# A fused attention and expert layer: the weighted sum over expert products moves from ScalarE and GpSimd to VectorE

## The chip, the cores and the metric

The kernel runs on one core of a Trainium2 chip. The metric is the device time of one execution in microseconds (us). Before the change three runs took 1968.68, 1968.94 and 1974.44 us; the median is 1968.94 us.

## The reference

For each of 16 sequences of 512 tokens with 128 channels, in fp32, the layer takes a layer norm `xn` of `x` and returns `x + attn(xn) + ffn(xn)`. Both branches hold an attention with 16 heads of 8 channels over all 512 tokens; the one in the second branch turns q and k by their position ("rope" below, the other is "plain"). The second branch then norms its own residual stream to `x1` and sends that through a shared expert and a routed sum:

```
shared = swiglu(x1 @ W_shared_in) @ W_shared_out
p_expert = softmax over the 4 experts of the best group * that group's probability
w[token, e] = p_expert for the 2 best experts of the token, else 0       # 8 experts
h = swiglu(x1 @ W1_shared)
routed = sum over e of (h @ W2_experts[e]) * w[:, e]
out = rmsnorm(x1 + shared + routed)
```

The change touches the last sum, `routed`: all eight products are computed, scaled by the token's weight and added.

## The kernel before, in words

**Passes.** The program is unrolled. For each batch `b` it runs an even pass and an odd pass of 64 quarters each (a quarter is one head times one block of 128 tokens). In each quarter TensorE issues one score product (L550) and one "shift" product (L565: the scores again, with the row's maximum taken off) of another attention. Behind every fourth quarter it issues a value product (L585). VectorE takes the row maximum of each score product straight from PSUM (L857, `maximum`); ScalarE exponentiates each shift product (L693, `weigh`) into `weights`, which has room for 8 heads. The even pass of batch b scores its plain attention and weighs the rope attention of b-1; the odd pass scores the rope attention of b and weighs the plain attention of b. Scores go through three PSUM banks, so score t needs the maximum of t-3 done.

**Clips.** The plain weights are clipped. GpSimd clips 12 of the 16 heads (L1048, 128x2048 in one instruction); VectorE clips heads 3, 7, 11 and 15, each in two halves of 128x1024 (L865) behind the maxima of quarters 17 and 18, 33 and 34, 49 and 50 of the odd pass and of quarters 1 and 2 of the next even pass.

**Side jobs.** All other products share one PSUM bank, `side_ps`. The lists EVEN and ODD say behind which quarter TensorE issues which job; each job waits until the one before it has been read out of the bank. In the even pass these are mostly the up and down products of the experts' hidden layer; in the odd pass `exp0` to `exp7`, two for each block of 128 tokens, each holding 4 experts x 128 channels (L657). LAG says for which batch: the experts run two batches behind the scores, so 14 odd passes have both (batches 2 to 15), and the last two sets of experts run behind the scores' end.

**Experts before.** When `expN` is done, ScalarE scales its four 128x128 quarters by the gate column into `spread` (L727, `weight_experts`: two in one quarter, two in the next, and the last frees the bank). GpSimd adds them up in three instructions (L1110, L1113, L1115, `mix`) into `out_sb`.

**Order.** Each engine runs its own queue in the order in which the program was written. AT says in which quarter the small steps stand (`invert`: the softmax denominators, L873 and L875; `top`, `shares`: the router's steps on VectorE; `square_x1`, `square_out`: VectorE's row sums of squares, L884). GpSimd's order is written out in its functions `even` and `odd`. A GpSimd step that belongs to the experts' result is the router (L1073 to L1102), which gives `gate`; `root` (L1032, L1035) gives the inverse root mean square; `third` (L1147) is the last part of a split of q or k into bf16 parts; `place_v` (L1024) and `divide` (L1133) serve the attention.

Of the kernel before, what the change touches and what calls it, by code (L numbers as in the profile page):

```python
# [39 lines left out]
NT = S // 128  # L40
# [22 lines left out]
EVEN = [("v0", [1]), ("x1T", [3]), ("max_rope1", [5]), ("v1", [8]), ("gates", [11]), ("up0", [13]), ("down0", [18]),  # L63
        ("up1", [21]), ("down1", [26]), ("up2", [28]), ("down2", [33]), ("up3", [36]), ("down3", [41]),
        ("shared_out", [45]), ("max_plain0", [49]), ("y_plain", [53])]
ODD = [("xnT", [0]), ("q_plain", [4]), ("k_plain", [9]), ("max_plain1", [11]), ("exp0", [14]), ("exp1", [17]),
# [9 lines left out]
AT = {"merge": 40, "invert": 28, "hi0": 8, "hi1": 11, "mid0": 11, "mid1": 24, "copy1": 18, "copy0": 52, "z": 28,  # L76
      "shares": 36, "top": 27, "square_x1": 47, "scale_x1": 53, "square_out": 5, "scale_out": 16, "stats": 36,
      "moments": 49, "act_x1T": 0, "act_max_rope1": 0, "act_up": 0, "act_max_plain0": 1, "act_v": 1,
      "act_max_plain1": 0, "act_xnT": 1, "act_q_plain": 1, "act_q_plain_2": 3, "act_k_plain": 0,
      "act_k_plain_2": 2, "act_exp": 0, "act_max_rope0": 0, "dve_gates": 0, "dve_up": 2, "dve_down": 1,  # L80
      "dve_y_plain": 1, "dve_shared_out": 0, "dve_q_plain": 2, "dve_k_plain": 1, "dve_y_rope": 3, "dve_job": 1,
      "act_exp_gap": 1}
# [66 lines left out]
def layer_kernel(nc, x, wq, wkcT, wk, wvcT, wvp, wvr, wo, w_up, w_out, w2, w_gate, bias, norms, consts, out):  # L149
    ctx = ExitStack()  # L150
    with ctx:
        def sb(name, shape, dt=F32):
            return ctx.enter_context(nc.sbuf_tensor(name, shape, dt))

        def sem(name):
            return ctx.enter_context(nc.semaphore(name))
# [79 lines left out]
        spread = sb("spread", [128, 2, 4, 128])  # L236
        two = sb("two", [128, 2, 128])
        one = sb("one", [128, 128])
# [76 lines left out]
        mixed = sem("mixed")  # L315
        rms_used = [sem("rms_used_x1"), sem("rms_used_out")]
# [367 lines left out]
        def _(act):  # L684
# [33 lines left out]
            def weight_experts(b, n, half):  # L718

                if live(b, -2):  # L720
                    if half == 0:
                        full(act, b, f"exp{n}")
                        act.wait_ge(route, cnt(b, -2, ROUTE_A + ROUTE_B, ROUTE_A + ROUTE_B))
                        if n >= 2:
                            act.wait_ge(mixed, cnt(b, -2, 24, 3 * (n - 2) + 1))
# [70 lines left out]
            def odd(b):  # L796
                for t in range(UNIT):
# [11 lines left out]
                    for n in range(8):  # L809
                        for half in range(2):  # L810
                            if t == after("odd", f"exp{n}", AT["act_exp"]) + AT["act_exp_gap"] * half:
                                weight_experts(b, n, half)
# [23 lines left out]
        def _(dve):  # L836
# [103 lines left out]
            def odd(b):  # L940
                for t in range(UNIT):
# [34 lines left out]
        def _(pool):  # L976
# [128 lines left out]
            def mix(b, n):  # L1105

                if live(b, -2):
                    taken(pool, b, f"exp{n}")
                    taken(pool, b, "shared_out")
                    pool.tensor_tensor(two[:], spread[:, n % 2, 0:2, :], spread[:, n % 2, 2:4, :],  # L1110
                                       ALU.add).then_inc(mixed, 1)
                    pool.wait_ge(mixed, cnt(b, -2, 24, 3 * n + 1))
                    pool.tensor_tensor(one[:, :], two[:, 0, :], two[:, 1, :], ALU.add).then_inc(mixed, 1)  # L1113
                    pool.wait_ge(mixed, cnt(b, -2, 24, 3 * n + 2))
                    pool.tensor_tensor(out_sb[:, n // 2, :], out_sb[:, n // 2, :], one[:, :], ALU.add).then_inc(mixed, 1)  # L1115
                    pool.wait_ge(mixed, cnt(b, -2, 24, 3 * n + 3))
# [63 lines left out]
            def even(b):  # L1180
                split_max(b, "max_rope1")
                square_out(b)
                turn(b, 0)
                turn(b, 1)
                rope_less_first(b, 0, q_rest, q_parts)
                root(b, -3, 1)
                rope_less_first(b, 1, k_rest, k_parts)
# [3 lines left out]
                third(b, 0, ROPE, 1, k_rest, k_parts)  # L1191
                split_max(b, "max_plain0")
                router(b, False)
                place_v(b, PLAIN)
                divide(b, PLAIN)
                spread_of_x(b)

            def odd(b):
                clip(b, 0)
                split_max(b, "max_plain1")  # L1200
                clip(b, 1)
                clip(b, 2)
                mix(b, 0)
                third(b, 1, PLAIN, 0, q_rest, q_parts)
                third(b, 1, PLAIN, 1, k_rest, k_parts)
                mix(b, 1)
                clip(b, 4)
                mix(b, 2)
                clip(b, 5)
                mix(b, 3)  # L1210
                mix(b, 4)
                clip(b, 6)
                clip(b, 8)
                divide(b, ROPE)
# [69 lines left out]
```

## Time and profile before

| | |
|---|---|
| median of three runs | 1968.94 us |
| profiled execution | 1971.31 us, its span 1969.5 us |
| TensorE busy | 1798.6 us (91%) |
| VectorE busy | 1633.5 us (83%) |
| ScalarE busy | 1446.3 us (73%) |
| GpSimd busy | 1180.6 us (60%) |
| chain that ended last, by engine | PE 55%, DVE 27%, SP's queue 7% |
| mean granted TensorE clock | 0.979 |

In the profile PE is TensorE, PEld its weight loads, DVE VectorE, ACT ScalarE, POOL GpSimd, SP the queue that issues transfers; L857 is line 857 of the kernel before. A busy time is a union of the instructions' spans. Instructions of one engine may overlap: VectorE's maxima take 0.68 us each and start 0.60 us apart.

### The profile page before, as it was taken

To read this page: it belongs to the slowest core of one execution; us is meant where nothing else is said; L and a number is where in the kernel's file an instruction comes from. 1 tells how busy PE (TensorE), PEld (TensorE's weight loads), DVE (VectorE), ACT (ScalarE), POOL (GpSimd) and SP (SyncE) were. 2 spreads that over 40 slices of the span, in tenths; PEclk is the share of its full clock that TensorE was granted. 3 is DMA by queue.
4 is the path that set the end of the run, shared out by engine and by line. 5 is a ranking of instruction groups with operands and counts; after the bars stand their busy time and mean duration, and the time that the engine had idled before them with its cause. 6 is when DMAs were issued, how large, how long until landed. Compare 5 with 4: busy or idle time off the path is not lost.

```text
span 1969.5 us, 33956 instructions
## 1 busy us (share of the span) xinstructions
PE 1798.6 (91%) x10244; PEld 526.8 (27%) x10244; DVE 1633.5 (83%) x2741; ACT 1446.3 (73%) x3095; POOL 1180.6 (60%) x1759
## 2 busy tenths in 40 slices
PE   5888899999999999999999999999999999999964
PEld 1122222222222232222222232222222222222222
DVE  4999998979899898989889898989989898987110
ACT  1378777778787788788777788777778887877622
POOL 3344548466674847567584856657485666738244
PEclk9899999999999999999999999999999999999977
DMA  4122222212122221212222121212222121220100
GB/s 123 31 64 73 72 70 59 76 56 84 57 63 76 60 80 56 84 57 71 70 58 81 57 81 57 82 57 59 81 61 78 56 85 57 62 69 28 45 25 6
DMA packets 120255, 126.34 MB, mean 64 GB/s; under 512 B 35196, under 2 KB 86780, under 8 KB 119932
## 3 DMA queue, kind: packets, MB, share of 16 engines
q1 hardware_dynamic: 119112, 123.39, 21.0%
q8 instruction: 81, 1.33, 0.3%
q10 hardware_dynamic: 960, 0.79, 0.2%
q14 instruction: 102, 0.84, 0.1%
HBM read 29.11 MB, written 22.02 MB: 26 GB/s over the span
## 4 chain that ended last, share of the span: by engine, by line
PE 55%; DVE 27%; SPq 7%; issue 4%; DMA 3%; ACT 3%; POOL 1%; POOLq 0%; ACTq 0%; DVEq 0%
DVE negmax L857 18%; PE score_ps L550 15%; PE o_ps L585 13%; PE side_ps L657 13%; SPq L394 6%; PE side_ps L644 4%; DVE weights L865 2%; PE side_ps L626 2%; PE side_ps L630 2%; PE side_ps L614 1%; DMA res_old<-res_new 1%; PE shift_ps L565 1%; PE side_ps L649 1%; DVE hidden L902 1%; PE side_ps L600 1%
## 5 line engine op out<-in xcount | busy, mean ns | idle before, releaser
L857 DVE TENSOR_REDUCE negmax<-score_ps 128x1 f32<-128x512 f32 x2048 | 1293.5, 681 | 167.5 <-PE score_ps L550 160.2
L693 ACT ACTIVATE weights<-shift_ps 128x512 f32<-128x512 f32 x2048 | 1114.2, 604 | 273.6 <-PE shift_ps L565 249.6
L550 PE MATMUL score_ps<-kt,qt 48*128 48x512 bf16 x2048 | 670.0, 394 | 74.6 <-DVE negmax L857 55.7
L565 PE MATMUL shift_ps<-qt,kt 51*128 51x512 bf16 x2048 | 655.8, 387 | 8.5 <-DMA qt<-max_rows 5.3
L585 PE MATMUL o_ps<-weights,vt 128*32 128x512 f32 x4096 | 551.4, 611 | 0.4 <-POOL weights L1048 0.4
L1048 POOL TENSOR_SCALAR weights<-weights 128x2048 f32<-128x2048 f32 x192 | 366.0, 1906 | 207.6 <-ACT weights L693 189.6
L550 PEld LDWEIGHTS score_ps<-kt,qt 48*128 48x128 bf16 x2048 | 148.7, 94 | 850.0 <-DVE negmax L857 746.8
L657 PE MATMUL side_ps<-w_sb,hidden 128*128 128x512 f32 x512 | 255.7, 622 | 18.6 <-ACT spread L727 14.0
L727 ACT ACTIVATE spread<-side_ps,gate 128x128 f32<-128x128 f32 x512 | 159.5, 372 | 134.2 <-PE side_ps L657 132.4
L644 PE MATMUL side_ps<-x1T,w_up_sb 128*128 128x512 f32 x256 | 151.7, 676 | 16.0 <-DVE hidden L902 8.6
L565 PEld LDWEIGHTS shift_ps<-qt,kt 51*128 51x128 bf16 x2048 | 150.3, 94 | 43.3 <-ACT weights L693 30.8
L1110 POOL TENSOR_TENSOR two<-spread 128x256 f32<-128x256 f32 x128 | 97.1, 759 | 97.2 <-ACT spread L727 59.7
L865 DVE TENSOR_SCALAR weights<-weights 128x1024 f32<-128x1024 f32 x128 | 137.0, 1071 | 0.0
L585 PEld LDWEIGHTS o_ps<-weights,vt 128*32 128x32 f32 x4096 | 81.3, 108 | 171.5 <-issue 159.3
L657 PEld LDWEIGHTS side_ps<-w_sb,hidden 128*128 128x128 f32 x512 | 87.4, 190 | 137.7 <-issue 62.6
L1115 POOL TENSOR_TENSOR out_sb<-out_sb,one 128x128 f32<-128x128 f32 x128 | 62.9, 491 | 10.0
L778 ACT ACTIVATE tanh<-side_ps 128x512 f32<-128x512 f32 x64 | 38.7, 605 | 36.0 <-PE side_ps L644 36.0
L1113 POOL TENSOR_TENSOR one<-two 128x128 f32<-128x128 f32 x128 | 58.2, 455 | 10.0
L626 PE MATMUL side_ps<-xnT,wq_sb 128*128 128x512 f32 x96 | 57.8, 686 | 2.8 <-DVE q_rest L954 1.4
L902 DVE SCALAR_TENSOR_TENSOR hidden<-tanh,side_ps 128x512 f32<-128x512 f32 x64 | 43.4, 679 | 20.3 <-ACT tanh L778 20.3
L1041 POOL TENSOR_TENSOR out_sb<-out_sb,norm_sb 128x512 f32<-128x512 f32 x16 | 20.4, 1275 | 64.0 <-ACT out_sb L737 64.0
L644 PEld LDWEIGHTS side_ps<-x1T,w_up_sb 128*128 128x128 f32 x256 | 39.7, 196 | 69.5 <-DVE hidden L902 36.0
(108 smaller groups left out, 1407.5 us busy)
## 6 DMA issues: line engine op xcount, KB each, us to landing
qt<-q_parts SPq DMA_DIRECT2D x768, 32.0 KB
kt<-k_parts SPq DMA_DIRECT2D x744, 32.0 KB
o_rows<-o_sb SPq DMA_DIRECT2D x64, 256.0 KB, 2.0
swung<-turned SPq DMA_DIRECT2D x64, 128.0 KB, 2.4
heads_raw<-o_rows SPq DMA_DIRECT2D x64, 128.0 KB
inv_wide<-inv_rows SPq DMA_DIRECT2D x32, 256.0 KB, 3.3
x_in<-in_x_dram SPq DMA_DIRECT2D x16, 256.0 KB, 3.5
xn_mid<-xn_new SPq DMA_DIRECT2D x16, 256.0 KB, 3.4
```

The source lines that it names most:

```text
L394: eng.dma_start(to[a][row:row + 8, 4 * gh:4 * gh + 4, :], parts[a][c:128:4, part[t], :]).then_inc(qk_landed[a][gh], 16)
L550: pe.matmul(score_ps[:, score_bank(a, t), :], qt[a][row:row + HROWS, slot, 128 * tile:128 * tile + 128], kt[a][row:row + HROWS, slot, :], ...
L565: pe.matmul(shift_ps[:, shift_bank(a, t), :], kt[a][row:row + HROWS + MROWS, slot, 128 * tile:128 * tile + 128], qt[a][row:row + HROWS + M ...
L585: mm = pe.matmul(o_ps[32 * j:32 * j + 32, :], vt[a][:, tile, 4 * (quad // 2) + j, 16 * ab:16 * ab + 32], weights[:, 4 * (quad % 2) + j, ti ...
L626: pe.matmul(to, w, xnT[:, :], start=True, stop=True).then_inc(side_full[at], 1)
L644: pe.matmul(to, w_up_sb[:, w, :], x1T[:, :], start=True, stop=True).then_inc(side_full[at], 1)
L657: mm = pe.matmul(to, hidden[:, 2 + c, 128 * tile:128 * tile + 128], w2_sb[:, c, 512 * e:512 * e + 512], start=(c == 0), stop=(c == 1))
L693: act.activation(weights[:, i % 8, tile, :], shift_ps[:, shift_bank(a, t), :], ACT.Exp, scale=SCALE).then_inc(weighed, 1)
L727: last = act.activation(spread[:, n % 2, e, :], bank(f"exp{n}")[:, 128 * e:128 * e + 128], ACT.Copy, scale=gate[:, n // 2, 4 * (n % 2) + e ...
L857: dve.tensor_reduce(negmax[:, i // 8, tile, i % 8:i % 8 + 1], score_ps[:, score_bank(a, t), :], AX.X, ALU.max, negate=True).then_inc(max_t ...
L865: dve.tensor_scalar(half, half, FLOOR, None, ALU.max).then_inc(clip_dve, 1)
L1048: pool.tensor_scalar(weights[:, i % 8], weights[:, i % 8], CEILING, FLOOR, ALU.min, ALU.max).then_inc(clip_pool, 1)
```

## The change

What it does: (1) ScalarE's scaling and GpSimd's three additions per `expN` go. VectorE reads the four 128x128 quarters from PSUM and adds each, times its gate column, to one of two running sums in SBUF: `out_sb` and a new tile `others`; half of it stands in the quarter of `expN`, half in the next. (2) GpSimd adds `others` to `out_sb` once per batch, in `join`, ahead of its squares. (3) VectorE's clips stay where they were. (4) Numbers in EVEN, ODD and AT move by one or two, `act_q_plain_2` by five, and GpSimd's `root`, `divide`, `split_max` and two of its clips change places.

```diff
-        spread = sb("spread", [128, 2, 4, 128])
-        two = sb("two", [128, 2, 128])
-        one = sb("one", [128, 128])
+        others = sb("others", [128, NT, 128])
...
-AT = {"merge": 40, "invert": 28, "hi0": 8, "hi1": 11, "mid0": 11, "mid1": 24, "copy1": 18, "copy0": 52, "z": 28,
-      "shares": 36, "top": 27, "square_x1": 47, "scale_x1": 53, "square_out": 5, "scale_out": 16, "stats": 36,
+AT = {"merge": 40, "invert": 27, "hi0": 8, "hi1": 11, "mid0": 12, "mid1": 26, "copy1": 18, "copy0": 52, "z": 30,
+      "shares": 37, "top": 27, "square_x1": 46, "scale_x1": 53, "square_out": 6, "scale_out": 18, "stats": 36,
...
-            def weight_experts(b, n, half):
-                        act.wait_ge(route, cnt(b, -2, ROUTE_A + ROUTE_B, ROUTE_A + ROUTE_B))
...
-                    for e in (2 * half, 2 * half + 1):
-                        last = act.activation(spread[:, n % 2, e, :], bank(f"exp{n}")[:, 128 * e:128 * e + 128],
-                                              ACT.Copy, scale=gate[:, n // 2, 4 * (n % 2) + e:4 * (n % 2) + e + 1])
...
+            def mix(b, n, half):
...
+                if half == 0:
+                    full(dve, b, f"exp{n}")
...
+                else:
+                    dve.wait_ge(mixed, cnt(b, -2, 8, n + 1))
...
+                dve.scalar_tensor_tensor(out=out_sb[:, tile, :], in0=product(0), scalar=share_of(0),
+                                         in1=out_sb[:, tile, :], op0=ALU.mult, op1=ALU.add)
+                if n % 2 == 0 and half == 0:
+                    last = dve.tensor_scalar(others[:, tile, :], product(1), share_of(1), None, ALU.mult)
+                else:
+                    last = dve.scalar_tensor_tensor(out=others[:, tile, :], in0=product(1), scalar=share_of(1),
+                                                    in1=others[:, tile, :], op0=ALU.mult, op1=ALU.add)
+                last.then_inc(mixed if half == 0 else free(f"exp{n}"), 1)
...
+                    for n in range(8):
+                        for half in range(2):
+                            if t == after("odd", f"exp{n}", AT["dve_exp"]) + half:
+                                mix(b, n, half)
...
-            def mix(b, n):
-
-                if live(b, -2):
-                    taken(pool, b, f"exp{n}")
...
+            def join(b):
+
+                if live(b, -3):
+                    taken(pool, b + (-1), "exp7")
+                    pool.tensor_tensor(out_sb[:], out_sb[:], others[:], ALU.add).then_inc(joined, 1)
+                    pool.wait_ge(joined, cnt(b, -3, 1, 1))
...
             def square_out(b):
                 if live(b, -3):
+                    join(b)
```

**VectorE, odd pass, from the y_rope addition (`x<-side_ps,xn_old`) to the clips of head 11.** Before:

```order
L880 TENSOR_TENSOR x<-side_ps,xn_old 128x512
L857 TENSOR_REDUCE negmax<-score_ps 128x1 x4
L884 TENSOR_REDUCE sums<-tanh 128x4
L857 TENSOR_REDUCE negmax<-score_ps 128x1 x2
L865 TENSOR_SCALAR weights<-weights 128x1024
L857 TENSOR_REDUCE negmax<-score_ps 128x1
L865 TENSOR_SCALAR weights<-weights 128x1024
```

Of the change, in the same place (`side_ps` holds `exp7`):

```order
L860 TENSOR_TENSOR x<-side_ps,xn_old 128x512
L837 TENSOR_REDUCE negmax<-score_ps 128x1 x3
L884 SCALAR_TENSOR_TENSOR out_sb<-side_ps,gate,out_sb 128x128
L889 SCALAR_TENSOR_TENSOR others<-side_ps,gate,others 128x128
L895 TENSOR_REDUCE sums<-tanh 128x4
L837 TENSOR_REDUCE negmax<-score_ps 128x1
L884 SCALAR_TENSOR_TENSOR out_sb<-side_ps,gate,out_sb 128x128
L889 SCALAR_TENSOR_TENSOR others<-side_ps,gate,others 128x128
L837 TENSOR_REDUCE negmax<-score_ps 128x1 x2
L845 TENSOR_SCALAR weights<-weights 128x1024
L837 TENSOR_REDUCE negmax<-score_ps 128x1
L845 TENSOR_SCALAR weights<-weights 128x1024
```

Four instructions of 128x128 come in, and the row sums of squares stand one maximum earlier.

**GpSimd, odd pass, from the squares of x1 (`tanh<-x`) to its norm weight.** Before:

```order
L1164 TENSOR_TENSOR tanh<-x 128x512
L1048 TENSOR_SCALAR weights<-weights 128x2048
L1024 COPY vt<-v_stage 128x32x8 x2
L1032 TENSOR_SCALAR sums<-sums 128x4
L1035 TENSOR_TENSOR rms<-sums,minus_half 128x4
L1048 TENSOR_SCALAR weights<-weights 128x2048
L1110 TENSOR_TENSOR two<-spread 128x256
L1113 TENSOR_TENSOR one<-two 128x128
L1115 TENSOR_TENSOR out_sb<-out_sb,one 128x128
L1041 TENSOR_TENSOR x<-x,norm_sb 128x512
```

Of the change:

```order
L1174 TENSOR_TENSOR tanh<-x 128x512
L1039 COPY vt<-v_stage 128x32x8 x2
L1047 TENSOR_SCALAR sums<-sums 128x4
L1050 TENSOR_TENSOR rms<-sums,minus_half 128x4
L1063 TENSOR_SCALAR weights<-weights 128x2048 x2
L1056 TENSOR_TENSOR x<-x,norm_sb 128x512
```

The clip of head 9 has gone behind the root and stands with that of head 10; the mix is gone.

**VectorE, even pass, around the denominators of the plain attention.** Before:

```order
L908 SCALAR_TENSOR_TENSOR hidden<-hidden,side_ps 128x512
L918 TENSOR_REDUCE top<-sel 128x4
L857 TENSOR_REDUCE negmax<-score_ps 128x1
L873 TENSOR_SCALAR den<-den 128x64
L875 RECIPROCAL inv_den<-den 128x64
```

Of the change:

```order
L919 SCALAR_TENSOR_TENSOR hidden<-hidden,side_ps 128x512
L853 TENSOR_SCALAR den<-den 128x64
L855 RECIPROCAL inv_den<-den 128x64
L929 TENSOR_REDUCE top<-sel 128x4
L837 TENSOR_REDUCE negmax<-score_ps 128x1 x3
```

The two steps on the denominators now stand ahead of `top`, for which GpSimd's router waits.

## Rows read from the trace of the kernel before

**Rows 1.** Windows of one steady batch: us, then busy (instructions) of PE, PEld, DVE, ACT, POOL

```profile
908.40:921.00 12.60, 12.38 (x80) 4.74 (x80) 11.44 (x19) 11.24 (x22) 9.30 (x12) 1.00 0.18 51
...
932.00:948.00 16.00, 15.20 (x91) 5.06 (x90) 15.93 (x33) 10.85 (x21) 7.31 (x25) 1.00 0.35 104
...
971.20:997.00 25.80, 25.80 (x126) 7.16 (x126) 20.24 (x31) 20.76 (x53) 19.89 (x22) 1.00 0.20 56
...
1004.60:1021.10 16.50, 13.39 (x87) 3.21 (x86) 15.93 (x25) 12.51 (x27) 15.33 (x16) 1.00 0.25 67
sum 112.70, PE 107.31 PEld 31.77 DVE 102.25 ACT 90.16 POOL 73.76; mean PE 13.41 PEld 3.97 DVE 12.78 ACT 11.27 POOL 9.22
```

**Rows 2.** Groups by line and shape: count, busy us, mean ns, idle before them

```profile
L857 DVE TENSOR_REDUCE negmax<-score_ps 128x1 f32<-128x512 f32 x2048 | 1293.5, 681 | 167.5 <-PE score_ps L550 160.2
L865 DVE TENSOR_SCALAR weights<-weights 128x1024 f32<-128x1024 f32 x128 | 137.0, 1071 | 0.0
...
L933 DVE BATCH_NORM_STATS2 stats<-x_in 128x6 f32<-128x128 f32 x64 | 17.5, 278 | 0.8 <-DMA x_in<-in_x_dram 0.6 <-issue 0.2
...
L727 ACT ACTIVATE spread<-side_ps,gate 128x128 f32<-128x128 f32 x512 | 159.5, 372 | 134.2 <-PE side_ps L657 132.4
...
L1110 POOL TENSOR_TENSOR two<-spread 128x256 f32<-128x256 f32 x128 | 97.1, 759 | 97.2 <-ACT spread L727 59.7 <-issue 33.3 <-POOL out_sb L1115 0.8
...
L1159 POOL TENSOR_TENSOR out_sb<-out_sb,res_old 128x512 f32<-128x512 f32 x16 | 20.3, 1267 | 1.3
```

**Rows 3.** Timeline of one expert product in the odd pass: start, length, engine

```profile
982.93 1.98 PE L657 MATMUL side_ps<-w_sb,hidden 128*128 128x512 f32 x4
984.85 0.39 PE L550 MATMUL score_ps<-kt,qt 48*128 48x512 bf16 x1
...
986.92 0.70 PE L657 MATMUL side_ps<-w_sb,hidden 128*128 128x512 f32 x1
...
985.27 1.29 DVE L857 TENSOR_REDUCE negmax<-score_ps 128x1 f32<-128x512 f32 x2 [1.16 <-PE score_ps L550]
...
984.96 0.62 ACT L727 ACTIVATE spread<-side_ps,gate 128x128 f32<-128x128 f32 x2 [0.90 <-PE side_ps L657]
```

**Rows 4.** Timeline of the odd pass behind exp7: TensorE, VectorE, GpSimd

```profile
1004.63 0.39 PE L550 MATMUL score_ps<-kt,qt 48*128 48x512 bf16 x1
...
1011.48 0.39 PE L550 MATMUL score_ps<-kt,qt 48*128 48x512 bf16 x1 [1.11 <-DVE negmax L857]
...
1005.06 0.69 DVE L857 TENSOR_REDUCE negmax<-score_ps 128x1 f32<-128x512 f32 x1 [0.60 <-PE score_ps L550]
...
1007.58 0.69 DVE L865 TENSOR_SCALAR weights<-weights 128x1024 f32<-128x1024 f32 x1
...
1008.78 2.05 DVE L865 TENSOR_SCALAR weights<-weights 128x1024 f32<-128x1024 f32 x1
1010.75 2.47 DVE L857 TENSOR_REDUCE negmax<-score_ps 128x1 f32<-128x512 f32 x4
...
1006.99 1.31 POOL L1035 TENSOR_TENSOR rms<-sums,minus_half 128x4 f32<-128x4 f32 x1
1008.39 1.89 POOL L1048 TENSOR_SCALAR weights<-weights 128x2048 f32<-128x2048 f32 x1
```

**Rows 5.** Timeline of the even pass around the denominators: VectorE, GpSimd, TensorE

```profile
932.81 1.16 DVE L873 TENSOR_SCALAR den<-den 128x64 f32<-128x64 f32 x1
...
932.37 0.21 POOL L1082 TENSOR_TENSOR z<-sel,top 128x16 f32<-128x16 f32 x1 [2.38 <-DVE top L918]
932.77 1.16 POOL L1147 TENSOR_TENSOR q_parts<-q_rest,q_parts 128x512 bf16<-128x512 f32 x1 [0.18 <-POOL z L1082]
...
932.27 1.13 PE L644 MATMUL side_ps<-x1T,w_up_sb 128*128 128x512 f32 x2 [0.21 <-DVE hidden L908]
```

**Rows 6.** Timeline behind the last scores: exp7 of batch 14 and the squares' sums

```profile
1890.49 3.65 PE L657 MATMUL side_ps<-w_sb,hidden 128*128 128x512 f32 x4 [0.88 <-DVE x L880]
...
1891.65 0.69 DVE L884 TENSOR_REDUCE sums<-tanh 128x4 f32<-128x512 f32 x1 [1.22 <-POOL tanh L1164]
```

More of the change, by code:

```diff
@@ L60 @@
 DEN = 8 * S // 128
-EVEN = [("v0", [1]), ("x1T", [3]), ("max_rope1", [5]), ("v1", [8]), ("gates", [11]), ("up0", [13]), ("down0", [18]),
-        ("up1", [21]), ("down1", [26]), ("up2", [28]), ("down2", [33]), ("up3", [36]), ("down3", [41]),
+EVEN = [("v0", [1]), ("x1T", [3]), ("max_rope1", [6]), ("v1", [8]), ("gates", [11]), ("up0", [13]), ("down0", [18]),
+        ("up1", [21]), ("down1", [26]), ("up2", [28]), ("down2", [32]), ("up3", [36]), ("down3", [41]),
         ("shared_out", [45]), ("max_plain0", [49]), ("y_plain", [53])]
-ODD = [("xnT", [0]), ("q_plain", [4]), ("k_plain", [9]), ("max_plain1", [11]), ("exp0", [14]), ("exp1", [17]),
+ODD = [("xnT", [1]), ("q_plain", [4]), ("k_plain", [9]), ("max_plain1", [11]), ("exp0", [14]), ("exp1", [17]),
        ("exp2", [21]), ("exp3", [25]), ("exp4", [29]), ("exp5", [33]), ("exp6", [37]), ("y_rope", [40]),
@@ L315, in layer_kernel @@
         mixed = sem("mixed")
+        joined = sem("joined")
         rms_used = [sem("rms_used_x1"), sem("rms_used_out")]
@@ L808, in odd @@
                     part(b, 1, t, "k_plain", after("odd", "k_plain", AT["act_k_plain_2"]), PLAIN, k_rest[:, :], k_parts, False)
[L809 to L812, printed above, removed]
                     if t == AT["copy1"]:
@@ L880, in add_side, with product, share_of @@
                 dve.tensor_tensor(dst, tiles(bank(job)), other, ALU.add).then_inc(free(job), 1)
+            def mix(b, n, half):
+                if not live(b, -2):
+                    return
+                tile, e = n // 2, 2 * half
+                if half == 0:
+                    full(dve, b, f"exp{n}")
+                    if n == 0:
+                        dve.wait_ge(route, cnt(b, -2, ROUTE_A + ROUTE_B, ROUTE_A + ROUTE_B))
+                        need(dve, joined, cnt(b, -2, 1, 0))
+                        taken(dve, b, "shared_out")
+                    else:
+                        taken(dve, b, f"exp{n - 1}")
+                else:
+                    dve.wait_ge(mixed, cnt(b, -2, 8, n + 1))
+                def product(k):
+                    return bank(f"exp{n}")[:, 128 * (e + k):128 * (e + k) + 128]
+                def share_of(k):
+                    return gate[:, tile, 4 * (n % 2) + e + k:4 * (n % 2) + e + k + 1]
+                dve.scalar_tensor_tensor(out=out_sb[:, tile, :], in0=product(0), scalar=share_of(0),
+                                         in1=out_sb[:, tile, :], op0=ALU.mult, op1=ALU.add)
+                if n % 2 == 0 and half == 0:
+                    last = dve.tensor_scalar(others[:, tile, :], product(1), share_of(1), None, ALU.mult)
+                else:
+                    last = dve.scalar_tensor_tensor(out=others[:, tile, :], in0=product(1), scalar=share_of(1),
+                                                    in1=others[:, tile, :], op0=ALU.mult, op1=ALU.add)
+                last.then_inc(mixed if half == 0 else free(f"exp{n}"), 1)
             def mean_square(b, which, lag):
@@ L1103, in router @@
                 assert k[0] == ROUTE_A + ROUTE_B
-            def mix(b, n):
-                if live(b, -2):
-                    taken(pool, b, f"exp{n}")
[L1109 to L1116, printed above, removed]
+            def join(b):
[3 more added lines that the diff above has]
+                    pool.wait_ge(joined, cnt(b, -3, 1, 1))
             def turn(b, n):
@@ L1194, in even @@
                 place_v(b, PLAIN)
-                divide(b, PLAIN)
                 spread_of_x(b)
             def odd(b):
+                split_max(b, "max_plain1")
                 clip(b, 0)
-                split_max(b, "max_plain1")
                 clip(b, 1)
-                clip(b, 2)
-                mix(b, 0)
                 third(b, 1, PLAIN, 0, q_rest, q_parts)
                 third(b, 1, PLAIN, 1, k_rest, k_parts)
-                mix(b, 1)
+                clip(b, 2)
                 clip(b, 4)
-                mix(b, 2)
                 clip(b, 5)
-                mix(b, 3)
-                mix(b, 4)
                 clip(b, 6)
+                divide(b, ROPE)
                 clip(b, 8)
-                divide(b, ROPE)
                 split_max(b, "max_rope0")
-                mix(b, 5)
                 square_x1(b)
-                clip(b, 9)
                 place_v(b, ROPE)
                 root(b, -1, 0)
+                clip(b, 9)
                 clip(b, 10)
-                mix(b, 6)
                 norm_weight(b, x1, 0, -1, x1_done)
-                mix(b, 7)
                 clip(b, 12)
```

18 lines of the change are left out of this document (6 added, 12 removed).

## Prediction

> **What bounds the kernel now.** I read the busy table and the chain of waits on the page, then windows over one steady batch, then the groups by shape, then the timelines of single places. The chain names TensorE and VectorE and hardly anyone else. The windows show why [rows 1]: in a batch of 112.70 us TensorE is busy for 107.31 and VectorE for 102.25, while ScalarE has 22 us and GpSimd 39 us to spare. The two change places. In the stretch of exp0 to exp6 (971.20 to 997.00) TensorE is busy for all of 25.80 us and VectorE for 20.24. Behind exp7 (1004.60 to 1021.10) VectorE is busy for 15.93 of 16.50 and TensorE for 13.39; there TensorE waits for maxima, up to 1.11 us at once [rows 4]. So the change takes work from two engines that bound nothing (ScalarE's scalings are 159.5 us in 512 instructions [rows 2]) and puts 512 instructions on one that bounds about half of each batch. What it costs depends on where in the batch they fall.
>
> **The price of one added instruction.** The trace has no multiply-and-add of 128x128 from PSUM. Nearest rows: the statistics of 128 columns take 278 ns, a maximum of 512 columns from PSUM 681 [rows 2], and four maxima in a row end after 2.47 us [rows 4]. So maxima start (2.47 - 0.68)/3 = 0.60 us apart. A column costs (681 - 278)/384 = 1.05 ns, so the spacing for 128 columns is 0.60 - 384 x 1.05 ns = 0.20 us. That is the lower bound; 0.28, with nothing overlapped, is the upper. I take 0.20, since VectorE's queue of independent instructions does overlap in these rows. A pair (half an expN) is then 0.40 us, an expN 0.80 us, a batch 6.4 us.
>
> The Trainium skill, "VectorE: DVE Perf Modes", section on the TRN2 errata, gives 120 cycles plus one per column from PSUM to SBUF at 0.96 GHz, and advises tiles of 512 or more since each instruction pays the fixed part. By it 128 columns would be 0.258 us, an estimate from that page, and the sum below would be some 0.7 us a batch higher, about 1996. The trace agrees with its 512-column figure as a duration (658 ns against 681), but the starts are 0.60 us apart, so part of that fixed cost is hidden here.
>
> **exp0 to exp6: mostly hidden, 0.4 us a batch.** Take one expN whose product ends at T = 984.85, when the next score starts [rows 3]. TensorE starts the next expN at 986.92, T+2.07, 3.99 us behind the last start and without a gap. VectorE idles for 1.16 us until the score lands at T+0.42. ScalarE picks the product up at T+0.11, and I let VectorE do so too. The first pair then runs to T+0.51, the maximum to 1.11, the second pair to 1.51, and the bank is free half a microsecond before TensorE wants it. Over the 3.99 us VectorE has four maxima and an expN, 2.4 + 0.8 = 3.2. That costs nothing, and what hides it is this idle time. Were it gone, each expN would cost up to 0.8 us. For exp1 and exp5 the clips of heads 3 and 7 stand between the pairs: at 0.60 undisturbed, the second pair ends at T+2.11, with the hand-over about T+2.25, 0.2 us too late each. That gives 0.4 in all. Bounds: 0 and, if GpSimd holds up the clips as below, about 2.0.
>
> **exp7, on the path: +0.36 us.** Here T = 1004.63 [rows 4]. Before, VectorE idled for 0.60 us and its next maximum started at 1005.06; the first clip half of head 11 started at 1007.58. Now: first pair 1004.74 to 1005.14, the sums to 1005.74, a maximum to 1006.34, second pair to 1006.74, two maxima to 1007.94. The clip starts 0.36 us later. Bounds: 0 (all in idle time) and 0.8.
>
> **The clips of head 11: +0.94 us.** The second half took 2.05 us, the first 0.69, though they are the same instruction [rows 4]. The long one started 0.39 us behind a GpSimd clip (1008.39, 1.89 us long) and ended 0.55 us behind that clip's end. The mean of all 128 halves is 1071 ns [rows 2]. So a clip half waits for a GpSimd instruction under way and then needs 0.55 us. In the changed order GpSimd's clips of heads 9 and 10 stand back to back directly behind the root. The sums end at about 1005.8; a hand-over, the small product and the power (1.31 at most [rows 4]) put the clip of head 9 at 1007.3 to 1007.6, just ahead of 1007.94. The first half then waits to about 1009.3 and lets the next maximum start at 1009.75. The GpSimd clip of head 10 starts as the first half releases it, near 1009.7, and runs to 1011.6; the second half, due at 1010.35, lets the next maximum start at 1012.05. Before, that was 1010.75 [rows 4]. 1.30 in all, less the 0.36 above: 0.94. Bounds: -1.37 (no collision at all) and +2.15 (both halves wait through a whole GpSimd clip, 2 x 2.36 against 2.57 before). I take the walk's value, which is nearest to the row at 1008.78.
>
> **The denominators: -0.55 us.** The addition on 128x64 took 1.16 us because GpSimd had started a split of 1.16 us 0.04 us before it, released by `top` through `z` [rows 5]. Now it stands ahead of `top`, so GpSimd waits at that point (2.38 us before [rows 5]) and the addition should cost about 0.2: VectorE is ahead by 0.98. But TensorE was busy for 15.20 of the 16.00 us from 932 on [rows 1], and 0.21 of the 0.80 idle lies before the place [rows 5]. It can be pulled ahead by some 0.55 to 0.59. Bounds: -0.98 and 0.
>
> **The rest: 0.** The join is a GpSimd addition like L1159, 1.27 us [rows 2], at the even pass's start. It pushes the router back, which has the 2.38 us wait for `top` as its cover [rows 5]; without it VectorE would stand at `top` for what is missing. The clip of head 15 beside the join, and the moved side jobs there, fall where TensorE is busy for 12.38 of 12.60 us [rows 1]; at most 0.2 either way. ScalarE's 10 us a batch less and GpSimd's mixes (the first of three additions alone is 759 ns [rows 2]) shorten nothing, since neither is waited for. The later ScalarE split steps have that same room.
>
> **Behind the last scores: +1.** The row sums of squares now stand behind the first pair of exp7. For batch 14 exp7 ran from 1890.49 to 1894.1 and the sums at 1891.65 [rows 6]; they become late by 3 us, of which ScalarE's wait for its own exp7 scalings had already taken about half: +1.6. The last join replaces three additions and gives back about 0.5.
>
> **Sum.** 0.40 + 0.36 + 0.94 - 0.55 = 1.15 us a batch, 14 odd passes with scores and experts: 16.1, and 1.0 at the end: 17.1. The profiled execution of 1971.31 us would become 1988.4. It lies 2.37 above the median of the runs, so against 1968.94 the time is 1986.
>
> **The rivals.**
> - *VectorE pays more.* Each instruction takes 0.28 us of the queue: 0.08 x 4 at exp7 and 0.08 x 8 at exp1 and exp5 add 0.96 a batch; 2.11 x 14 + 1 = 30.5, 1999. For it: the instructions are short and each starts on an operand pair from PSUM and SBUF. Against it: the 0.60 us spacing.
> - *The clips of head 11 come free.* GpSimd has lost its mixes; if the clip of head 9 starts only after the first half, or both GpSimd clips are done before it, no half meets one: -1.37 in place of +0.94. It decides at about 0.5 us between GpSimd's clip 9 and VectorE's clip. The batch is then 0.40 + 0.36 - 1.37 - 0.55 = -1.16, the sum -16.2 + 1, and the time 1954: faster. For it: margins of 0.3 to 0.6 us. Against it: two GpSimd clips of 1.89 us in a row can't both miss two halves 0.6 us apart.
> - *Nothing changes.* One half still collides as before (0 in place of 0.94), and the 0.55 pays for exp7 and half of the stalls: 0.36 + 0.20 - 0.55 = 0, 1969. That is also the case in which VectorE's idle time takes up all that is added, as the change would have it.
>
> **Chances and range.** Forecast 0.42 (own range 1974 to 1998), VectorE pays more 0.18, clips free 0.25, nothing 0.15. A measurement can tell about 0.3%, 5.9 us, from no change. Faster by more than that: 0.25 + 0.01 of the third rival, 0.26; within: 0.13 of that rival and 0.05 of the forecast's low side, 0.18; slower: 0.56. The range from 1952 to 2006 takes in the second rival and the first with a stall or two more; all low ends together would be 33 us under, all high ones 69 us over, and I leave those out.
>
> **What would show it.** In the changed profile: the added instructions at 0.2 us of spacing; expN starts 3.99 us apart but for exp1 to exp2 and exp5 to exp6 (4.2); both halves of head 11's clip at about 1.9 us; the addition on the denominators near 0.2 us; a batch of about 113.9 us. If head 11's halves are short, or the batch is under 112.7, the forecast is wrong there; if expN starts are over 4.2 apart throughout, VectorE's idle time did not hide the pairs.

## The result, and the profile after

The changed kernel takes 2002.58 us (median of 4 runs, 2000.17 to 2003.68); the kernel before took 1969.36 beside it (4 runs). The ratio is 1.0161, interval 1.0141 to 1.0181: slower, by 1.6%. The forecast was 1986, the range 1952 to 2006. The profiled execution took 2003.68 us, 32.4 more than the one before.

The page of the changed kernel, its busy table and the chain by engine:

```profile
PE 1805.1 (90%) x10244; PEld 523.3 (26%) x10244; DVE 1751.8 (88%) x3253; ACT 1327.0 (66%) x2583; POOL 975.6 (49%) x1391
...
DVE 45%; PE 42%; SPq 5%; issue 4%; DMA 2%; ACT 1%; POOL 1%; POOLq 0%; DVEq 0%; ACTq 0%
```

The work moved as the change says: GpSimd is 205 us less busy, ScalarE 119 us, VectorE 118 us more. TensorE's busy time hardly changed, but its share of the chain fell from 55% to 42%, and VectorE's rose from 27% to 45%.

VectorE's costliest groups by line and shape (count, busy us, mean ns, idle before them). L837 is the maxima, L845 the clip halves, L884 and L889 the added multiply-and-adds:

```profile
L837 DVE TENSOR_REDUCE negmax<-score_ps 128x1 f32<-128x512 f32 x2048 | 1294.0, 681 | 73.6 <-PE score_ps L548 67.2
L845 DVE TENSOR_SCALAR weights<-weights 128x1024 f32<-128x1024 f32 x128 | 140.2, 1096 | 0.0
L884 DVE SCALAR_TENSOR_TENSOR out_sb<-side_ps,gate,out_sb 128x128 f32<-128x128 f32 x256 | 88.9, 347 | 67.5 <-PE side_ps L655 66.0
L889 DVE SCALAR_TENSOR_TENSOR others<-side_ps,gate,others 128x128 f32<-128x128 f32 x192 | 65.7, 342 | 0.0
```

The maxima cost what they cost before [rows 2]. Their idle time fell from 167.5 to 73.6 us, and the added groups have an idle time of their own. So a good part of the new work did fall into VectorE's waits, and yet the kernel is slower: the loss is local. Windows of one steady batch of the changed kernel show where (us, then busy of PE, PEld, DVE, ACT, POOL, and the granted clock). The first two are the even and the odd pass, each from its first maximum to that of the next pass; then the denominators and exp0 to exp6, as in [rows 1]. The last one goes from the start of exp7 to the pass's end; the window in [rows 1] begins 1.9 us later, when exp7 is done, so the same stretch of the kernel before is given below:

```profile
926.92:979.07 52.15, 50.73 (x326) 15.95 (x326) 49.61 (x92) 42.43 (x84) 28.09 (x57) 1.00 0.26 81
979.07:1041.45 62.38, 56.69 (x318) 15.65 (x316) 59.06 (x112) 40.36 (x77) 32.64 (x29) 1.00 0.20 56
...
950.50:966.50 16.00, 15.30 (x92) 5.17 (x94) 15.15 (x33) 10.80 (x21) 8.32 (x25) 1.00 0.36 110
...
989.05:1015.90 26.85, 25.97 (x126) 7.15 (x126) 25.26 (x56) 15.40 (x29) 13.29 (x10) 1.00 0.18 53
...
1021.65:1041.45 19.80, 15.49 (x90) 3.88 (x90) 19.44 (x32) 12.43 (x25) 14.00 (x11) 1.00 0.22 59
```

Before, the same batch (even pass, odd pass, and from the start of exp7):

```profile
908.38:961.21 52.83, 51.06 (x326) 16.25 (x326) 50.72 (x92) 42.39 (x84) 27.46 (x57) 1.00 0.26 80
961.22:1021.07 59.85, 56.23 (x318) 15.50 (x317) 51.51 (x80) 47.77 (x109) 46.29 (x53) 1.00 0.21 58
...
1002.72:1021.07 18.35, 15.24 (x90) 3.86 (x90) 17.64 (x28) 13.33 (x29) 17.01 (x17) 1.00 0.24 66
```

The even pass gained 0.68, the odd one lost 2.53: +1.85 a batch where 1.15 was forecast. From the start of exp7 on VectorE is now busy for 19.44 of 19.80 us (19.79 without the rounding of the edges) instead of 17.64 of 18.35, and from exp0 to exp6 for 25.26 of 26.85, where it had 5.6 us to spare [rows 1].

**One expN in the clear.** TensorE's and VectorE's timeline: the starts of exp2, exp3, exp5 and exp6, and VectorE at exp3 and exp5 (start, length; in brackets the idle time before and what ended it), to be laid beside [rows 3]:

```profile
997.25 1.98 PE L655 MATMUL side_ps<-w_sb,hidden 128*128 128x512 f32 x4 [0.35 <-DVE others L889]
1001.24 1.98 PE L655 MATMUL side_ps<-w_sb,hidden 128*128 128x512 f32 x4
...
1009.21 1.98 PE L655 MATMUL side_ps<-w_sb,hidden 128*128 128x512 f32 x4
...
1013.80 1.98 PE L655 MATMUL side_ps<-w_sb,hidden 128*128 128x512 f32 x4 [0.53 <-DVE others L889]
...
1003.26 0.35 DVE L884 SCALAR_TENSOR_TENSOR out_sb<-side_ps,gate,out_sb 128x128 f32<-128x128 f32 x1 [0.47 <-PE side_ps L655]
1003.53 0.34 DVE L889 SCALAR_TENSOR_TENSOR others<-side_ps,gate,others 128x128 f32<-128x128 f32 x1
1003.79 0.68 DVE L837 TENSOR_REDUCE negmax<-score_ps 128x1 f32<-128x512 f32 x1
...
1011.28 0.35 DVE L884 SCALAR_TENSOR_TENSOR out_sb<-side_ps,gate,out_sb 128x128 f32<-128x128 f32 x1
1011.54 0.35 DVE L889 SCALAR_TENSOR_TENSOR others<-side_ps,gate,others 128x128 f32<-128x128 f32 x1
1011.79 0.69 DVE L837 TENSOR_REDUCE negmax<-score_ps 128x1 f32<-128x512 f32 x1
1012.39 0.83 DVE L845 TENSOR_SCALAR weights<-weights 128x1024 f32<-128x1024 f32 x1
1013.15 0.34 DVE L884 SCALAR_TENSOR_TENSOR out_sb<-side_ps,gate,out_sb 128x128 f32<-128x128 f32 x1
1013.41 0.34 DVE L889 SCALAR_TENSOR_TENSOR others<-side_ps,gate,others 128x128 f32<-128x128 f32 x1
```

From exp3 (1001.24) to exp5 (1009.21) the starts are 3.98 and 3.99 us apart, as before: the pairs are hidden there. VectorE even idles for 0.47 us ahead of the pair at 1003.26. The price is read from the starts: 1003.26, 1003.53, 1003.79, so 0.53 us a pair, 0.26 to 0.27 an instruction. At exp5 the clip half of head 7 stands between the maximum and the second pair. The bank comes free at the end of the instruction at 1013.41, TensorE has waited 0.53 us, and exp6 starts 4.59 us behind exp5. Between exp1 (992.85) and exp2 it is 4.40, with a wait of 0.35 us.

**Behind exp7.** VectorE, GpSimd and TensorE at the clips of head 11, answering to [rows 4]:

```profile
1027.10 1.81 DVE L845 TENSOR_SCALAR weights<-weights 128x1024 f32<-128x1024 f32 x1
...
1029.43 1.77 DVE L845 TENSOR_SCALAR weights<-weights 128x1024 f32<-128x1024 f32 x1
...
1026.47 4.19 POOL L1063 TENSOR_SCALAR weights<-weights 128x2048 f32<-128x2048 f32 x2
...
1029.57 0.39 PE L548 MATMUL score_ps<-kt,qt 48*128 48x512 bf16 x1 [1.21 <-DVE negmax L837]
...
1031.86 0.39 PE L548 MATMUL score_ps<-kt,qt 48*128 48x512 bf16 x1 [0.85 <-DVE negmax L837]
```

Both halves are long now (1.81 and 1.77 against 0.69 and 2.05), each beside one of GpSimd's two clips, and TensorE waits for the maximum behind each. That is the collision as forecast.

**The denominators.** VectorE and GpSimd, answering to [rows 5]: the addition takes 0.19 us instead of 1.16.

```profile
950.47 0.19 DVE L853 TENSOR_SCALAR den<-den 128x64 f32<-128x64 f32 x1
...
951.35 0.21 POOL L1097 TENSOR_TENSOR z<-sel,top 128x16 f32<-128x16 f32 x1 [2.05 <-DVE top L929]
```

**The ramp, not foreseen.** The ramp is the first passes, before the experts run; odd pass 1 has no experts yet. It took 59.11 us against 54.25, and the even pass ahead of it 1.8 us more than before, with a mean granted clock of 0.96 instead of 1.00. Odd pass 1 of the changed kernel, then of the kernel before (windows; the group of clip halves in that window):

```profile
174.80:233.90 59.10, 47.73 (x284) 11.39 (x282) 54.07 (x79) 40.15 (x77) 32.62 (x29) 0.88 0.21 59
...
L845 DVE TENSOR_SCALAR weights<-weights 128x1024 f32<-128x1024 f32 x6 | 10.1, 1682 | 0.0
```

```profile
172.90:227.10 54.20, 44.78 (x285) 11.17 (x285) 47.97 (x79) 39.34 (x77) 33.06 (x29) 0.97 0.23 68
...
L865 DVE TENSOR_SCALAR weights<-weights 128x1024 f32<-128x1024 f32 x6 | 4.1, 683 | 0.0
```

Four of the six halves run into GpSimd's clips there, none did before: 6.0 us of VectorE, and the mean granted clock of the pass falls from 0.97 to 0.88.

**The tail.** The squares' sums of batch 14 stand behind the first pair of exp7 (TensorE starts exp7 at 1922.81) and start 2.55 us behind it, where they started 1.16 behind [rows 6]:

```profile
1925.36 0.68 DVE L895 TENSOR_REDUCE sums<-tanh 128x4 f32<-128x512 f32 x1
```

The tail is 0.8 us longer.

So the 32.4 us are: the first passes +6.7, the odd passes from 2 on +33.9, the even ones from 2 on -9.1, the ends +0.9.

### The profile page after: what moved, and what is told of

It reads as the page before. It is cut to its first block, busy times and chain, and to the rows that moved or that the text cites. A ratio compares the mean times of both kernels' runs of the same rounds, so it can differ in the third digit from the quotient of the medians.

```text
span 2001.9 us, 33431 instructions
## 1 busy us (share of the span) xinstructions
PE 1805.1 (90%) x10244; PEld 523.3 (26%) x10244; DVE 1751.8 (88%) x3253; ACT 1327.0 (66%) x2583; POOL 975.6 (49%) x1391
## 4 chain that ended last, share of the span: by engine, by line
DVE 45%; PE 42%; SPq 5%; issue 4%; DMA 2%; ACT 1%; POOL 1%; POOLq 0%; DVEq 0%; ACTq 0%
DVE negmax L837 27%; PE score_ps L548 11%; PE side_ps L655 9%; PE o_ps L583 8%; DVE weights L845 6%; PE side_ps L642 5%; SPq L392 4%; DVE out_sb L884 3%; PE side_ps L624 2%; DVE others L889 2%; PE side_ps L647 1%; PE side_ps L628 1%; DVE hidden L919 1%; DVE hidden L913 1%; PE shift_ps L563 1%
## 5 line engine op out<-in xcount | busy, mean ns | idle before, releaser
L837 DVE TENSOR_REDUCE negmax<-score_ps 128x1 f32<-128x512 f32 x2048 | 1294.0, 681 | 73.6 <-PE score_ps L548 67.2
L884 DVE SCALAR_TENSOR_TENSOR out_sb<-side_ps,gate,out_sb 128x128 f32<-128x128 f32 x256 | 88.9, 347 | 67.5 <-PE side_ps L655 66.0
L845 DVE TENSOR_SCALAR weights<-weights 128x1024 f32<-128x1024 f32 x128 | 140.2, 1096 | 0.0
L1142 POOL TENSOR_TENSOR headsT<-heads_raw,inv_wide 128x512 f32<-128x512 f32 x32 | 40.9, 1280 | 154.6 <-DMA inv_wide<-inv_rows 147.9
L1020 POOL CAST max_parts<-negmax 128x32 bf16<-128x32 f32 x64 | 13.7, 214 | 127.2 <-DVE negmax L837 126.2
L889 DVE SCALAR_TENSOR_TENSOR others<-side_ps,gate,others 128x128 f32<-128x128 f32 x192 | 65.7, 342 | 0.0
L1156 POOL TENSOR_TENSOR q_parts<-q_rest,q_parts 128x512 bf16<-128x512 f32 x32 | 37.0, 1158 | 53.5 <-ACT q_parts L742 51.0
L700 ACT ACTIVATE max_rows<-side_ps 24x512 bf16<-24x512 bf16 x64 | 37.1, 580 | 32.2 <-PE side_ps L605 32.2
```

What stands on the lines that cost most here:

```text
L837: dve.tensor_reduce(negmax[:, i // 8, tile, i % 8:i % 8 + 1], score_ps[:, score_bank(a, t), :], AX.X, ALU.max, negate=True).then_inc(max_t ...
L845: dve.tensor_scalar(half, half, FLOOR, None, ALU.max).then_inc(clip_dve, 1)
L884: dve.scalar_tensor_tensor(out=out_sb[:, tile, :], in0=product(0), scalar=share_of(0), in1=out_sb[:, tile, :], op0=ALU.mult, op1=ALU.add)
L889: last = dve.scalar_tensor_tensor(out=others[:, tile, :], in0=product(1), scalar=share_of(1), in1=others[:, tile, :], op0=ALU.mult, op1=AL ...
```

## The experiments

Theory: the changed kernel loses at two places. Clip halves on VectorE run into GpSimd's clips (head 11, and the ramp), and at exp1 and exp5 a clip half stands ahead of the second pair and so holds up TensorE's bank. Rivals: VectorE is simply full (+118 us busy); or the new numbers in the tables cost the time, not the products.

**e1. GpSimd's clips of heads 9 and 10 earlier** (changed kernel; GpSimd's order only):

```
 max_rope0 split
+clip(b, 9)
 square_x1, place_v
+clip(b, 10)
 root(b, -1, 0)
-clip(b, 9)
-clip(b, 10)
```

> The changed kernel with GpSimd's clip of head 9 moved ahead of its squares of x1 and the clip of head 10 ahead of the root, so that no GpSimd clip is under way when VectorE clips head 11. Theory (the loss is mostly VectorE's clip halves of head 11 waiting for GpSimd's clips 9 and 10): both halves fall from 1.8 us to 0.69, an odd pass from 62.4 to about 60.1, 14 x 2.3 = 32 us less, about 1970. Rival (VectorE is simply full, whatever its order): the wait comes back at another place, over 1990. Rival (the moved numbers in the tables are the loss): no change, 2002.

1963.07 us; ratio to before 0.9957 (0.9939 to 0.9974). The clip halves of head 11 on VectorE, and GpSimd beside them:

```profile
1010.77 0.68 DVE L845 TENSOR_SCALAR weights<-weights 128x1024 f32<-128x1024 f32 x1
...
1011.97 0.68 DVE L845 TENSOR_SCALAR weights<-weights 128x1024 f32<-128x1024 f32 x1
...
1007.15 1.89 POOL L1063 TENSOR_SCALAR weights<-weights 128x2048 f32<-128x2048 f32 x1
...
1009.41 1.03 POOL L1050 TENSOR_TENSOR rms<-sums,minus_half 128x4 f32<-128x4 f32 x1
```

Both halves are at 0.68 us, and exp7 to the pass's end shrinks from 19.79 to 17.57. With the same instructions on VectorE the kernel is 39.5 us faster, more than the whole loss; a part of that is a collision that the kernel before had too (e6). The odd passes from 2 on take 38 us less together. The ramp isn't mended: odd pass 1 falls from 59.11 to 57.01, but odd pass 0 grows from 52.22 to 55.07, and the first two batches take 202.5 us against 201.7.

**e2. Half the products' additions** (changed kernel without the additions to out_sb; one half of the routed experts' sum is left out, so its time is that of less work):

```
-dve.scalar_tensor_tensor(out=out_sb[:, tile, :], in0=product(0), scalar=share_of(0),
-                         in1=out_sb[:, tile, :], op0=ALU.mult, op1=ALU.add)
```

> The changed kernel without the multiply-and-adds into out_sb: only the two experts per product that go to the second running sum are added, so half of the routed sum is left out and VectorE runs 256 instructions of 128x128 fewer. Theory (an added instruction costs only where VectorE is waited for: two pairs at exp1, exp5 and exp7, 0.26 us each): about 0.5 us less at each of the three, 1.5 us a batch, about 1981. Rival (VectorE is full, each added instruction costs its 0.26 us): 16 x 0.26 = 4.2 us a batch, 59 us, about 1944. Rival (the moved numbers): about 2000.

1980.1 us; ratio 1.0038 (1.002 to 1.0055). 256 instructions of 0.26 us, 67 us of VectorE, are gone; 22.5 us come back. The odd pass of batch 8 is 61.12 us against 62.38. A full VectorE is refuted: two thirds of what was removed had been hidden.

**e3. The kernel before, with the addition on the denominators one step earlier** (invert 28 becomes 27, nothing else):

> The kernel before with one number changed: the softmax denominators stand in quarter 27 instead of 28, ahead of the step for which GpSimd's router waits. Theory (the addition on 128x64 waited 1 us for a GpSimd split, and TensorE can be pulled ahead by 0.5 to 0.7): the addition falls from 1.16 to 0.19 us, an even pass from 52.8 to about 52.2, 14 x 0.6 = 9 us less, about 1960. Rival (the even pass's gain in the changed kernel comes from the other moved numbers or the lost mixes): 1969.

1961.97 us; ratio 0.9949 (0.9929 to 0.9968). All sixteen additions (min/median/max in ns; the median was 1162):

```profile
L873 DVE TENSOR_SCALAR den<-den x16: 184/188/195, 149.5 to 1828.4; 128x64 f32<-128x64 f32 x16
```

Its even passes are mostly 52.18 us (batch 8: 52.00) against 52.83: one number of the tables gives about 0.65 us a batch by itself.

**e4. The changed kernel with the tables and GpSimd's order of before:**

```
-"max_rope1", [6] ... "down2", [32] ... "xnT", [1];  invert 27, mid0 12, mid1 26, z 30 ...
+"max_rope1", [5] ... "down2", [33] ... "xnT", [0];  invert 28, mid0 11, mid1 24, z 28 ...
```

> The changed kernel with the tables EVEN, ODD and AT and GpSimd's written order of the kernel before (the mixes taken out of that order, the join kept in). Theory: the denominators' 0.6 us a batch come back, one half of head 11 still waits for GpSimd's clip 10 but the other not, so about +0.6 - 1.1 = -0.5 us a batch against the changed kernel: about 1995, still above 1969. Rival (the moved numbers are the loss): about 1970. Rival (VectorE is full): about 2010.

1992.31 us; ratio 1.0119 (1.0086 to 1.0152). Batch 8: even 52.65, odd 61.37. Of the loss of 1.6%, 1.2% stay, so the moved numbers and the new GpSimd order aren't its main cause; with them the changed kernel is 10 us slower still. Behind exp7 one collision (18.94 us, 1.37 over e1's 17.57) becomes two (19.79), and odd pass 1, where no half is long in e4, goes from 53.15 to 59.11; together that is more than the even passes give back. So the second collision at head 11 and those of odd pass 1 come with the new numbers and order, not with the work that GpSimd lost: e4 has lost it too, and it has one collision at head 11, as before.

**e7. As e1, and the second pair ahead of the second clip half on VectorE:**

```
-if t > 16 and t % 16 in (1, 2):
-    clip(b, t // 4 - 1, t % 16 - 1)
+if t > 16 and t % 16 == 1:
+    clip(b, t // 4 - 1, 0)
 ... mix(b, n, half) ...
+if t > 16 and t % 16 == 2:
+    clip(b, t // 4 - 1, 1)
```

> The kernel with the early GpSimd clips (1963 us), and in VectorE's order the second pair of an expert product stands ahead of the second clip half of heads 3, 7 and 11. Theory (exp1 and exp5 each free the side bank some 0.4 to 0.5 us too late, because a clip half stands between their pairs): the products start 3.99 us apart throughout, about 0.9 us a batch less, 13 us, about 1950. Rival (VectorE is full over the batch and pays wherever the clip stands): 1963.

1948.67 us; ratio 0.9876 (0.9847 to 0.9905). TensorE at exp5 and exp6, and the second clip half of head 7, now behind the pair that ends at 984.06:

```profile
980.27 1.99 PE L655 MATMUL side_ps<-w_sb,hidden 128*128 128x512 f32 x4
...
984.26 1.98 PE L655 MATMUL side_ps<-w_sb,hidden 128*128 128x512 f32 x4
...
983.98 0.73 DVE L845 TENSOR_SCALAR weights<-weights 128x1024 f32<-128x1024 f32 x1
```

All starts from exp1 to exp6 are 3.98 to 3.99 us apart again. The odd pass of batch 8 is 59.26 (most are 59.21), 1.0 us under e1, as the theory has it.

**e6. The kernel before with the edits of e1 and e3** (its own expert scalings and mixes; GpSimd's clips of 9 and 10 earlier; invert 27):

> The kernel before with the denominators in quarter 27 and GpSimd's clips of heads 9 and 10 ahead of its squares and its root. Theory (in the kernel before, too, the second half of head 11's clip waits 1.4 us for a GpSimd clip, in a stretch where TensorE waits for VectorE): 14 x 1.3 = 18 us under the 1962 of the kernel with the denominators alone, about 1944. Rival (GpSimd's mixes take the place of the clip in the collision, or hold up the early clips): 1955 to 1962.

1946.62 us; ratio 0.9857 (0.9821 to 0.9894). Its odd pass of batch 8, and the last stretch ahead of the tail's end:

```profile
947.74:1006.22 58.48, 56.24 (x318) 15.58 (x317) 50.06 (x80) 47.48 (x109) 45.46 (x53) 1.00 0.21 60
...
1768.00:1850.00 82.00, 76.47 (x369) 20.61 (x366) 24.93 (x40) 52.77 (x111) 29.14 (x55) 0.85 0.10 33
```

Rid of its own collision at head 11, before runs a batch in 110.47 us, 1.93 less than e1 and 0.93 less than e7. In the profiled executions e7 and e6 are alike only because the tail of e6 is 11 us longer, with the clock at 0.85 on average where before had 0.98; that execution was the slowest of e6's six, which go from 1933.17 to 1950.23 us. So moving the products to VectorE, with the numbers that moved along, costs 1.93 us a batch at e1's order and 0.93 at e7's. Nothing here shows it gaining by itself.

**e5. All clips on GpSimd** (as e1, and VectorE's 8 halves a batch become 4 clips of 128x2048 in GpSimd's order):

> The changed kernel with VectorE's clips of heads 3, 7, 11 and 15 given to GpSimd, one instruction of 128x2048 each, and with GpSimd's early clips of heads 9 and 10. Theory (what is lost is the collision of the two engines' clips and the clip halves between the pairs): no collision and no clip half left, against the changed kernel 1.0 us at exp1 and exp5 and 3.6 us at head 11 less, 4.6 x 14 = 64 us, about 1940. Rival (GpSimd then comes late with head 11 for the value products, or TensorE bounds the rest of the odd pass): 1950 to 1965. Rival (VectorE's multiply-and-adds themselves bound): over 1970.

1937.04 us; ratio 0.982 (0.9787 to 0.9853): the fastest kernel of these, ahead of both. Odd pass 58.51 us, batch 110.61:

```profile
946.20:1004.71 58.51, 56.42 (x318) 15.46 (x316) 53.17 (x105) 39.93 (x77) 38.05 (x32) 1.00 0.21 59
```

Its batch is 0.14 us longer than e6's. Of the 10.9 us between the two profiled executions 7 lie in the tail and 4 in the odd passes, of which e6 has longer ones, so its lead isn't one of the steady batch.

**e8. The same clips with the experts still on ScalarE and GpSimd** (kernel before, invert 27, all clips on GpSimd):

> The kernel before (experts scaled by ScalarE and added by GpSimd) with the denominators in quarter 27, the early GpSimd clips, and VectorE's clips of heads 3, 7, 11 and 15 given to GpSimd. It stands beside the changed kernel with all clips on GpSimd (1937 us): what differs is who makes the weighted sum. Theory (freed of collisions, the sum's place costs or gives little, since exp0 to exp6 run at TensorE's pace either way): 1.0 to 1.5 us a batch less than with VectorE's clips at head 11, about 1930, within 10 us of 1937. Rival (GpSimd now has too much and comes late with clips or mixes): over 1950.

1996.9 us; ratio 1.0123 (1.0085 to 1.016). My forecast missed by 67 us; the rival held. A GpSimd that still mixes comes late with the clips. Three clips back to back on GpSimd in batch 8, and TensorE's loads of clipped weights that wait for them (us in total, times, longest, over the whole run); behind it the same wait in the kernel before:

```profile
999.65 5.84 POOL L1035 TENSOR_SCALAR weights<-weights 128x2048 f32<-128x2048 f32 x3 [0.22 <-POOL out_sb L1102]
...
PEld o_ps L583 <- POOL weights L1035: 55.1, 44, 2.0
```

```profile
PEld o_ps L585 <- POOL weights L1048: 6.7, 15, 0.7
```

TensorE now waits for GpSimd's clips, up to 2.0 us at once. So the time that the change frees on GpSimd is worth something where GpSimd has all clips (1996.9 against 1937.0; the other moved numbers differ too), but the change as it stands doesn't spend it, and e6, with the clips on both engines, runs the same batch as e5 without it.

## Why the prediction was right in direction and short in size

The walk behind exp7 can be taken apart by four kernels, from the start of exp7's product to the pass's end: before 18.35 us, before without collision 16.98 (e6), changed 19.79, changed without collision 17.57 (e1). The windows of e6 and e1:

```profile
989.24:1006.22 16.98, 15.25 (x90) 3.96 (x90) 16.27 (x28) 13.00 (x29) 15.14 (x17) 1.00 0.27 69
...
1005.32:1022.89 17.57, 15.48 (x90) 3.93 (x90) 17.21 (x31) 11.96 (x25) 11.79 (x10) 1.00 0.26 67
```

e4 against before, with one collision each, gives the same price of exp7's products: 18.94 - 18.35 = 0.59.

| term, us a batch | forecast | measured | from |
|---|---|---|---|
| exp1 and exp5 | +0.40 | +1.02 | starts 4.40 and 4.59 against 3.98 and 3.99 |
| exp7's products | +0.36 | +0.59 | 17.57 - 16.98 |
| clips of head 11 | +0.94 | +0.85 | (19.79 - 17.57) - (18.35 - 16.98) |
| denominators | -0.55 | -0.67 | even passes (mostly -0.66 to -0.68) |
| rest | 0 | +0.07 | the other starts, 0.02 to 0.03 each |
| batch | +1.15 | +1.86 | windows: +1.85 |
| ends | +1 once | +0.9 once | head and tail |
| first passes | 0 | +6.7 once | odd pass 1 and the even pass ahead |

**The price, the step that failed.** "I take 0.20" should have been 0.26. I derived it by scaling the overlap of 512-column maxima down to 128 columns, and the starts above show 0.26 to 0.27. The Trainium skill, "VectorE: DVE Perf Modes", section on the TRN2 errata (120 cycles plus one per column from PSUM, 0.258 us as an estimate), was right for this spacing, and I set it aside. Its sum, 1996, was nearer to 2002.58; with the 6.7 us of the ramp it would be about 2003. Of the branches the rival "VectorE pays more" came nearest (0.28 us an instruction, 1999, chance 0.18): 2002.58 lies outside the forecast's own range of 1974 to 1998. Its reason, the operand pair from PSUM and SBUF, the trace doesn't bear out: L887, which reads one tensor, from PSUM, keeps the queue for 0.26 us as well (999.54 to 999.80).

**exp1 and exp5** were mis-sized for that reason and two more. At exp5 the product ends at T = 1011.13. I had the second pair end at T+2.11; it ended at T+2.62. The four instructions take 0.24 of the difference, the clip half 0.16 (0.83 long while GpSimd divides the heads, 1011.40 to 1012.68), and the last one counts with its length of 0.34, not with its spacing. The mechanism stood: e7 takes the clip half out from between the pairs, and both starts are back at 3.99 us.

**The clips of head 11** came as walked: both halves long, GpSimd's clip of head 9 starting 0.63 us ahead of the first. e1 is the rival "come free" made true: from 19.79 to 17.57, 2.22 us where the rival had 2.31. The forecast rested here on a rule read from two rows (a clip half waits for the GpSimd instruction under way, then needs 0.55 us), and it holds again: the clip of head 9 ended about 1028.36 (its start and 1.89 us), the half at 1028.91. The Trainium skill, "SBUF — State Buffer", "Who interferes with whom", says that VectorE in its two-port modes, which a `tensor_scalar` such as the clip can enter, shares a pair of ports with GpSimd, and that whoever issues first holds it for the whole instruction; the halves of 0.68 and 1.81 us agree with that.

**The denominators** gained a little more than forecast; e3 (-0.65) shows the gain needs none of the rest of the change.

**The ramp** was left out. I counted only passes that have scores and experts. In odd pass 1 the products are missing but the new order of GpSimd's clips is not, and there four halves collide.

**Behind the last scores** the size (+0.8 where +1 was forecast) is luck. I had the sums 3 us late; they start 1.4 us later behind the start of exp7 than before. In the profile before, exp7 of batch 14 took 3.65 us [rows 6], nearly all of it at the lower of the clock's two levels, 1.2 GHz; in the changed kernel it took 1.98 at the full one.

**The clock** makes some passes longer. In odd pass 4 TensorE waits 1.21 and 0.85 us behind exp7 as in batch 8, and then the granted clock falls to its lower level, 1.2 GHz, for some 7 us (windows from exp7 to the end of the first of the two waits, and from there to the pass's end):

```profile
560.10:568.00 7.90, 6.33 (x36) 1.70 (x36) 7.62 (x14) 4.89 (x10) 5.93 (x7) 1.00 0.09 26
568.00:581.90 13.90, 12.08 (x54) 2.38 (x54) 12.03 (x19) 7.54 (x16) 8.06 (x5) 0.75 0.26 68
```

From exp7 to its end that pass took 21.77 us instead of 19.79. Another 1.4 us it lost at its start, at the full clock, where TensorE waited for a transfer; 65.85 in all:

```profile
516.97 0.39 PE L563 MATMUL shift_ps<-qt,kt 51*128 51x512 bf16 x1 [1.04 <-DMA qt<-max_rows]
```

Not every long pass is the clock's: odd pass 13 took 64.03 us at the full clock. Before has long passes too (62.88 and 61.77 against 59.85). Over odd passes 2 to 14 the time above the shortest one is 12.1 us, 9.1 before, so about 3 of the 32.4 us are of this kind. The waits of 1.21 and 0.85 us stand in all thirteen of these passes, and the clock falls behind exp7 in five. In the profiles of e1, e5 and e7, which don't have these two waits, the granted clock is 1.00 in every odd pass from 2 on; in e6, which doesn't have them either, it falls in two. Why it falls in some passes and not in others stays open, as does the long tail of e6.

## What to carry to other kernels

Before work moves onto an engine that "has room", lay its instructions into the timeline of each place and ask what stands ahead of the one that frees a buffer: here the 3.99 us from one expN to the next hid both pairs fully, except where a clip stood between them. Price an added instruction by the spacing of starts of its own shape, and where no row has the shape, let the forecast go by the upper bound. When the order of an engine's instructions changes, look at which instructions of another engine they now run beside, in the ramp as well as in the steady state: the change as it stood cost 33 us, and moving two GpSimd clips gave 39.5 us in the changed kernel (e1) and 15.4 in the kernel before (e6 against e3).

## What the runs showed that I had not expected

- The products on VectorE don't meet GpSimd: the pair at 1011.28 and 1011.54 took 0.35 us each beside a GpSimd multiplication that ran from 1011.40 to 1012.68, while the clip half beside the same instruction took 0.83. In the whole trace those that began beside a GpSimd instruction have the same median, 0.34 to 0.35 us, as the others.
- An addition of 128x64 on VectorE costs 0.19 us or 1.16, by whether a GpSimd split started 0.04 us ahead of it.
- Taking 119 us from ScalarE and 205 from GpSimd gained nothing in the steady batch that any run here shows: e5, which gives GpSimd other work, runs it in 110.61 us, e6, which has the sum where it was, in 110.47.
